# Sums of exponentials over keys: three tiles added together ahead of one set of sums, in a layer of attention and experts

## The reference

```python
xn = _layernorm(x)
q, k = _apply_rope(q, k)                        # q, k, v: (8, 16, 512, 32) from xn
scores = einsum('bhqd,bhkd->bhqk', q, k) / sqrt(32)
scores = where(causal, scores, finfo.min)
attn = softmax(scores, axis=-1)
out = einsum('bhqk,bhkd->bhqd', attn, v)        # then @ Wo.T
# experts: top 2 of 8 by xn @ gate_w.T, y = xn @ W_e.T + b_e, weighted sum of the two
return x + attention(xn) + experts(xn)
```

## Time and profile before

| | us |
|---|---|
| runs shown (3) | 1005.15, 1007.92, 1008.72 |
| median | 1007.92 |
| the profiled execution | 1008.12 |
| its span, first to last instruction | 1006.3 |

### The profile page before, as it was taken

The page is one execution under the profiler, slowest core; times in us unless marked ns, Lnnn a source line. Parts: engine busy times, 40 slices in busy tenths (PEclk is TensorE's granted clock), DMA queues, the critical chain, the costliest instruction groups (busy, mean ns, idle before and its releaser), DMA issues.

```text
span 1006.3 us, 18752 instructions
## 1 busy us (share of the span) xinstructions
PE 932.0 (93%) x6589; PEld 447.7 (44%) x6589; DVE 743.2 (74%) x1322; ACT 435.2 (43%) x711; POOL 565.7 (56%) x557
## 2 busy tenths in 40 slices
PE   2899989989999978988999999989999999999887
PEld 1344434434444433444555555544444444444333
DVE  7888988888889899543444444477878888788865
ACT  5367866666765432331211211214433444334442
POOL 1545675664676548572333333237887788777651
PEclk9999999999999999998999999999999999999999
DMA  6366588788785352385555555554555554455431
GB/s 238 106 220 223 146 278 311 204 300 292 206 291 209 117 210 85 134 309 177 179 168 176 179 170 174 168 214 142 184 159 176 191 191 148 148 181 179 157 107 54
DMA packets 107964, 188.63 MB, mean 187 GB/s; under 512 B 11873, under 2 KB 65249, under 8 KB 102625
## 3 DMA queue, kind: packets, MB, share of 16 engines
q1 hardware_dynamic: 97072, 152.03, 44.5%
q0 software_dynamic: 10800, 35.40, 12.3%
HBM read 117.13 MB, written 70.25 MB: 186 GB/s over the span
## 4 chain that ended last, share of the span: by engine, by line
PE 67%; DVE 12%; DMA 7%; POOL 6%; ACT 4%; issue 3%; SPq 1%; another core or an unknown queue 0%; DVEq 0%; ACTq 0%; POOLq 0%
PE psum L942 18%; PE psum L1027 11%; PE psum L1036 6%; PE psum L1051 6%; PE psum L990 6%; PE psum L977 5%; PE psum L959 5%; PE psum L993 5%; DMA x_in<-x 3%; PE psum L919 3%; DVE top L1463 3%; PE psum L961 2%; POOL gT L571 1%; DMA c_rows<-c_turn 1%; POOL y_in L616 1%
## 5 line engine op out<-in xcount | busy, mean ns | idle before, releaser
L756 ACT ACTIVATE pT<-psum,factors 128x512 f32<-128x512 f32 (+1 forms) x352 | 219.6, 640 | 267.6 <-PE psum L977 239.3
L1463 DVE TENSOR_REDUCE top<-psum 128x1 f32<-128x384 f32 (+3 forms) x352 | 210.7, 635 | 24.1 <-PE psum L961 23.1
L1027 PE MATMUL psum<-xT,w_att 128*128 128x512 f16 x768 | 199.0, 385 | 6.9 <-DVE xT L1414 4.8
L942 PE MATMUL psum<-w_exp,x_gT 128*128 x852 | 197.4, 382 | 0.8 <-DVE x_gT L1419 0.6
L959 PE MATMUL psum<-k_stack,q_stack 96*128 96x384 f16 (+3 forms) x512 | 129.1, 305 | 22.2 <-DVE top L1463 21.4
L606 POOL DMA_INDIRECT x_g<-xn_rows,tok_of x71 | 67.3, 948 | 143.8 <-PE psum L919 136.4
L977 PE MATMUL psum<-q_stack,k_stack 98*128 98x256 f16 (+3 forms) x512 | 129.5, 306 | 6.3 <-ACT pT L756 5.0
L1419 DVE TENSOR_TENSOR x_gT<-psum,x_gT 128x512 f16<-128x512 f32 x71 | 49.0, 692 | 106.9 <-ACT x_gT L780 94.4
L942 PEld LDWEIGHTS psum<-w_exp,x_gT 128*128 128x128 f16 x852 | 83.9, 98 | 87.4 <-issue 3.9
L780 ACT ACTIVATE x_gT<-psum 128x512 f16<-128x512 f32 x71 | 42.3, 597 | 173.2 <-PE psum L919 173.1
L590 POOL TENSOR_SCALAR_AFFINE_SELECT pT<-pT 128x512 f32<-128x512 f32 x128 | 99.3, 785 | 18.7 <-ACT pT L756 18.7
(11 more groups left out here) (172 smaller groups left out, 1283.9 us busy)
## 6 DMA issues: line engine op xcount, KB each, us to landing
y_rows<-y_sb SPq DMA_DIRECT2D x71, 256.0 KB
w_in<-w_all SPq DMA_DIRECT2D x12, 1024.0 KB, 9.6
q_stack<-qk_rows SPq DMA_DIRECT2D x96, 128.0 KB
k_stack<-qk_rows SPq DMA_DIRECT2D x96, 128.0 KB
x_in<-x SPq DMA_DIRECT2D x8, 1024.0 KB, 13.5
qk_rows<-q_hl SPq DMA_DIRECT2D x32, 256.0 KB, 2.2
qk_rows<-k_hl SPq DMA_DIRECT2D x32, 256.0 KB
xn_rows<-x_in SPq DMA_DIRECT2D x8, 1024.0 KB, 4.7
```

The lines of the kernel that those rows point to most:

```text
L756: act.activation(p_of(j, h, heads), banks[BANK_T + (NT_ * n + k) % 2][:, 0:W], ACT.Exp, scale=factors[:, 0:1]).then_inc(exp_done, 1)
L942: now = pe.matmul(banks[s % 4], x_gT[s % 4][:, xp * C + c, :], w_exp[:, bass.ds(e, 1), wp, c, :].rearrange("p e d -> p (e d)"), start=n == ...
L1027: now = pe.matmul(bank, w_att[:, what, wp, c, g * P:(g + 1) * P], xT[b % 2][:, xp * C + c, :], start=at_pass == 0, stop=at_pass == 3 * C - 1)
L1463: return dve.tensor_reduce(out=top[:, h:h + heads, i], in_=banks[BANK_S + k % 2][:, 0:heads * W].rearrange("p (h t) -> p h t", h=heads), a ...
```

## The change

`added(n)` is true for head groups 16 to 30. For these, TensorE makes the sums of tile 0 as before, and leaves the sums of tiles 1, 2 and 3 out of their places. VectorE adds `p_of(2)` and then `p_of(3)` into the right-hand columns of `p_of(1)` (`add_exps`, in the step after, between the second and the third score maximum), once the product of tile 1 with v is done and the tiles are masked. TensorE then makes one set of sums over the 384 columns of `p_of(1)`, behind the product of tile 3 with v, after a wait for VectorE (`p_added`). ScalarE's exponentials of tiles 1 to 3 wait for the whole head group before instead of the same tile of it. On GpSimd the low part of k moves, in steps from 16 on, from behind `mask(n, 1)` and the gathers to behind `mask(n, 3)`.

```diff
@@ -295,6 +295,11 @@
     LATE = [w for n in range(N) for w in late_tiles(n)]
     LATE_AT = {w: i for i, w in enumerate(LATE)}
     assert sorted(LATE) == list(range(NT))
+    def added(n):
+        return N1 <= n < N - 1
@@ -636,7 +641,7 @@
                 mask(n, 1)
                 if n >= N1 and n + 1 < N:
                     gather_y(late_tiles(n + 1)[1])
-                if n + 3 < N:
+                if n < N1:
                     low_qk(1, n + 3)
                 if n in TURN_AT:
                     low_x(TURN_AT[n], 0)
@@ -645,6 +650,8 @@
                 if n in TURN_AT:
                     low_x(TURN_AT[n], 2)
                 mask(n, 3)
+                if n >= N1 and n + 3 < N:
+                    low_qk(1, n + 3)
                 if n in TURN_AT:
                     low_x(TURN_AT[n], 3)
                 if n == CHOOSE + 2:
@@ -752,7 +759,7 @@
                 W = heads * (S - j * P)
                 act.wait_ge(t_done, NT_ * n + k + 1)
                 if n:
-                    act.wait_ge(pv_done, J * (n - 1) + j + 1)
+                    act.wait_ge(pv_done, J * n if added(n - 1) and j else J * (n - 1) + j + 1)
                 act.activation(p_of(j, h, heads), banks[BANK_T + (NT_ * n + k) % 2][:, 0:W], ACT.Exp,
                                scale=factors[:, 0:1]).then_inc(exp_done, 1)
@@ -978,6 +985,12 @@
                                     q_stack[u][0:ROW_C + 2, h0 + h, j * P:S], start=True, stop=True)
                 now.then_inc(t_done, 1)
+            def sums(n, j, last):
+                for h in range(HG):
+                    now = pe.matmul(banks[BANK_DEN][h * HD:(h + 1) * HD, j * P:S], ones32[:], p_of(j, h, 1),
+                                    start=j == 0, stop=j == last)
+                return now
             def times_v(n, j):
                 b, g = n // G, n % G
                 pe.wait_ge(masked, J * n + j + 1)
@@ -987,12 +1000,15 @@
                         pe.wait_ge(o_read, n)
                 W = S - j * P
                 for h in range(HG):
-                    pe.matmul(banks[BANK_O][h * HD:(h + 1) * HD, j * P:S], v_sb[b % 2][:, j, g * P + h * HD:g * P + (h + 1) * HD],
-                              p_of(j, h, 1), start=j == 0, stop=j == J - 1)
-                for h in range(HG):
-                    now = pe.matmul(banks[BANK_DEN][h * HD:(h + 1) * HD, j * P:S], ones32[:], p_of(j, h, 1),
-                                    start=j == 0, stop=j == J - 1)
-                now.then_inc(pv_done, 1)
+                    now = pe.matmul(banks[BANK_O][h * HD:(h + 1) * HD, j * P:S], v_sb[b % 2][:, j, g * P + h * HD:g * P + (h + 1) * HD],
+                                    p_of(j, h, 1), start=j == 0, stop=j == J - 1)
+                if not added(n) or j == 0:
+                    sums(n, j, J - 1).then_inc(pv_done, 1)
+                elif j < J - 1:
+                    now.then_inc(pv_done, 1)
+                else:
+                    pe.wait_ge(p_added, n - N1 + 1)
+                    sums(n, 1, 1).then_inc(pv_done, 1)
             def times_v_last(i, first, last):
@@ -1472,6 +1488,17 @@
                 own.link(dve.tensor_tensor(c_hl[:, 0, :], tops, c_scale[:], ALU.mult))
                 dve.tensor_tensor(c_hl[:, 1, :], c_f[:], c_hl[:, 0, :], ALU.subtract).then_inc(c_made, 1)
+            def add_exps(n):
+                dve.wait_ge(pv_done, J * n + 2)
+                for j in range(2, J):
+                    dve.wait_ge(masked, J * n + j + 1)
+                    W = S - j * P
+                    to = p_of(1).rearrange("p (h t) -> p h t", h=HG)[:, :, S - P - W:S - P]
+                    now = dve.tensor_tensor(to, to, p_of(j).rearrange("p (h t) -> p h t", h=HG), ALU.add)
+                    if j < J - 1:
+                        own.link(now)
+                now.then_inc(p_added, 1)
             def normalise_o(n):
                 dve.wait_ge(pv_done, J * (n + 1))
                 if n in JOB_AT:
@@ -1535,6 +1562,8 @@
                     largest_score(n + 1, 1)
                 if n in NORM_AT:
                     rstd_of(NORM_AT[n])
+                if n and added(n - 1):
+                    add_exps(n - 1)
                 if nxt:
                     largest_score(n + 1, 2)
                     largest_score(n + 1, 3)
```

More of the change, by code:

```diff
@@ L235, in moe_attention_layer @@
     c_loaded = [sem(f"c_loaded{u}") for u in range(3)]
-    t_done, exp_done, masked, pv_done = (sem(n) for n in ("t_done", "exp_done", "masked", "pv_done"))
+    t_done, exp_done, masked, pv_done, p_added = (sem(n) for n in ("t_done", "exp_done", "masked", "pv_done", "p_added"))
     o_read, o_hi, o_lo, wo_done, experts_done, sum_done = (sem(n) for n in ("o_read", "o_hi", "o_lo", "wo_done", "experts_done", "sum_done"))
```

## The result

| | before | after |
|---|---|---|
| median, us (4 runs each, side by side) | 1006.53 (1002.35 to 1008.72) | 1023.59 (1020.87 to 1026.57) |
| the profiled execution | 1008.12 | 1026.57 |
| its span | 1006.3 | 1024.8 |

A forecast was written before the change was run, and what follows sets the result against it. TensorE was taken as the bound, 21.05 us a step over another loop of 20.22. Step 17 +0.55, twelve loops +14.6, last steps +0.58 and +1.66: together 17.4 on 1008.1, giving 1025.5 us, range 1011 to 1035.

The forecast's parts named there:

- Step 1: On TensorE, sums of the third and fourth tiles go: 0.65 us a step in 15 steps, 9.8 us if TensorE stays bound.
- Step 2: On VectorE, the two inserted adds cost 1.95 us as a free pair.
- Step 3: VectorE's adds and GpSimd instructions run one after the other, the waiting engine next; the first add lasts over 1.5 us.
- Step 4: GpSimd's k low part, 1.16 us, precedes the second add either way; SyncE's stores leave 1 to 2 us later, hidden.
- The new loop: One normalise start to the next, through GpSimd's row, adds and two maxima: 22.2 us, with TensorE's own work at 20.40.
- The twelve loops: Normalise of step 17 to that of step 29: twelve loops of 22.2 us, 266.4 against 251.81, +14.6 us.
- the clock's rival: TensorE's clock falls at every new wait: 12 x 1.3 us on top, 1041 us; chance 0.13.
- Steps 30 and 31: Last steps, without rope or k: normalise later by 0.58 us in step 30 and 1.66 us in step 31.
- A sign that failed: TensorE's busy time over the kernel falls by some 10 us while the span grows.
- Step 17: First normalise behind the adds, with GpSimd already free: it starts at 694.45 instead of 693.90, +0.55 us.
- the adds are hidden: Rival: VectorE's adds are hidden and TensorE stays the bound, 998 us; chance 0.09.
- The port gives the adds their turn first: Rival: both VectorE adds go ahead of GpSimd's k low part, or overlap it: loop 21.09 us, total 1012; chance 0.13.

The follow-up runs named there:

- e3: The changed kernel with both adds cut to one column per head, waits and signals kept: 999.91 us, 0.9941 times before.
- e2: The changed kernel with GpSimd starting k's low part only when both adds are done: 1013.61 us, 1.0119 times before.
- e1: The changed kernel with k's low part put back ahead of the masks, adds kept: 1024.09 us, 1.0212 times before.
- e4: The kernel before with only the move of k's low part behind the masks, no adds: 1005.94 us, 1.0000 times before.
- e7: The kernel before with only GpSimd's second pair of gathers moved behind the masks, no adds: 1008.05 us, 0.9992 times before.
- e5: The changed kernel with GpSimd's second pair of gathers behind the masks and k's low part back ahead of them: 1010.54 us, 1.0022 times before.
- e9: As e2, but only the fourth tile is added and the third tile's sums stay on TensorE: 1004.94 us, 0.9983 times before.

## Why the prediction was right, and where it was off

The forecast was 1025.5 us for the profiled execution's 1008.1; it took 1026.57, and the median is 1023.59. The mechanism in a steady step was the forecast's; that the total came so close is in part luck, as the parts below show.

- **Step 1, sums removed:** e3's loop of 20.40 is the predicted 21.05 - 0.65.
- **Step 2, price of the adds:** free pair 1.95 predicted, 1.95 in the chain of e2. The group of second adds in after, over all 15 steps (busy us, mean ns, idle before), is the 692 ns of the earlier trace rows:

```profile
L1497 DVE TENSOR_TENSOR pT<-pT 128x512 f32<-128x512 f32 x15 | 10.4, 692 | 0.5
```

- **Step 3, the shared port:** right for the sum. From 700 to 920 us the first add averages 2.125 us in after and 1.250 in e2, where GpSimd is idle beside it (groups of instructions by form, first of after, then of e2):

```profile
L1497 DVE TENSOR_TENSOR pT<-pT 128x1024 f32<-128x1024 f32 x10 | 21.2, 2125 | 0.0
```
```profile
L1498 DVE TENSOR_TENSOR pT<-pT 128x1024 f32<-128x1024 f32 x10 | 12.5, 1250 | 0.0
```

  The Trainium skill (SBUF — State Buffer, section Summary: rules for kernel authors) has the second of such a pair to issue fully blocked until the first finishes. The timeline of the result agrees: the add issued 0.18 us behind the low part and ended 1.11 behind its end. But the prediction's reading that the engine that waited gets the next turn failed where it was put to the test: in the timeline of after, step 28, the add has waited since 956.59 behind a mask, and the low part queued behind that mask still goes first.

```profile
955.84 1.22 POOL L595 TENSOR_SCALAR_AFFINE_SELECT pT<-pT 128x512 f32<-128x512 f32 x2
956.59 3.41 DVE L1497 TENSOR_TENSOR pT<-pT 128x1024 f32<-128x1024 f32 x2 [0.37 <-POOL pT L595]
957.03 1.15 POOL L591 TENSOR_TENSOR k_hl<-plain_k,k_hl 128x512 f16<-128x512 f32 x1
960.05 1.51 PE L990 MATMUL psum<-pT,ones 128*32 128x384 f32 x8 [2.51 <-DVE pT L1497]
```

  By the chain the first add ends at 959.28, 1.10 behind the low part's end (958.18). The same happened in the step at 889. It changes nothing in the sum, since the low part stands once in the row either way, as step 4 had it.
- **Step 4, the low part stands in the row wherever it is put, and SyncE is hidden:** the first is shown by e1 (21.97 against 21.96), the second fits e4 (1.0000) and e2, where the low part comes later still.
- **The new loop:** 22.2 predicted, 21.96 in an undisturbed step. With the step above, whose N is 827.09 - 21.96 = 805.13, the gathers end at N + 16.81 (16.82 predicted) and the second add at N + 20.98 (946.49 - 925.49 = 21.00 predicted). The miss of 0.24 is the last term: two maxima and the gaps, 1.21 by the records, took 0.98, because a record overlaps its neighbour's on the same engine by some 0.1.
- **The twelve loops:** +14.6 predicted, +14.49 measured, but partly by cancelling: undisturbed loops would have given 12 x 21.96 - 251.81 = +11.7, and three disturbed ones, which the forecast did not have, added the rest. The match of the total is luck to that extent. In the first, a gather is issued 1 us late (timeline of after):

```profile
886.26 1.02 POOL L621 DMA_INDIRECT y_in<-y_rows,idx_y  x1 [1.31 <-issue]
892.76 0.85 PE L990 MATMUL psum<-pT,ones 128*32 128x384 f32 x8 [2.05 <-DVE pT L1497]
```

  Before has the same late issue at 877.57, hidden under TensorE. Now GpSimd is in the loop: 22.66, and TensorE waits 2.05 us. Behind that wait the granted clock is 0.50, that is 1.2 GHz (chain, and windows of 1 us, columns as above):

```profile
894.14 2.56 PE psum L1043 x6
...
894.00:895.00 1.00, 1.00 (x4) 0.38 (x3) 0.93 (x3) 0.69 (x1) 0.83 (x1) 0.50 0.64 214
```

  The half projection takes 2.56 instead of 1.30, and the next loop 23.36, 1.40 more than the ordinary: the price that the prediction gave the clock's rival (1.3). The third is step 28 above, where the sums themselves take 1.51 instead of 0.85 after a wait of 2.51. So the clock's rival is no mechanism of every step, as argued from the earlier trace rows: behind the ordinary wait of 1.34 (826.16) the half projection at 827.33 took its 1.30. It came behind the longer waits.
- **Steps 30 and 31:** the loop to N(30) is 0.38 longer than before's and the loop to N(31) 1.20, together 1.58; the forecast's sum has 0.58 + 1.66 = 2.24. The 1.66 was counted against before's N(31) with N(30) left in its place, so adding both counts 0.58 twice unless the masks move with N(30). They did not: they end at 994.02, 32.40 behind N(29), instead of 33.14. On the other side the sums ahead of N(31) took 1.46 instead of the 0.85 counted.
- **Not foreseen:** from N(31) to the end 27.41 instead of 26.40, 1.0 us. The granted clock is 0.50 from 996 to 999, behind two waits of TensorE close together, 1.11 for a mask and 1.39 for the adds; before's is 1.00 around its N(31). These are the sums and the next group (chain of after):

```profile
995.88 1.46 PE psum L990 x8
997.34 0.97 PE psum L984 x2
```

- **A sign that failed:** TensorE's busy time was to fall by some 10 us. It fell by 2.2 (929.8 against 932.0); in e3 it fell by 10.5 (921.5). The half clock, at which the same matmuls last longer, fits: of the 1 us windows from 690 us on, 15 of after have a granted clock of 0.50 and 7 of before, and from 664 to 690 us 6 and 2. How much of the 8 us it makes wasn't measured.
- **Step 17:** +0.55 was predicted; N(17) came 1.42 later, though the stage's first maxima came 1.72 earlier. Little of that is the change's. From the first maxima to N(17) the two kernels without adds differ by 2.7 us among themselves (30.92 in e4, 28.24 in e7); before has 28.26 and after 31.40. From `add_attention` on, where the adds are, the changed kernel is 0.89 longer (690.53 to 695.32, before 690.00 to 693.90). N(17) lies anywhere from 691.30 to 698.10 in the profiled executions of this document, so the 1.42 can't be put down to the change. Why the stage starts unevenly wasn't tried.

The parts add up: 1.42 + 14.49 + 0.38 + 1.20 + 1.01 = 18.50 us, the difference of the spans. The rivals: "the adds are hidden" fell, since even the free pair gives 21.10 (e2, e5); its stated point of decision, adds of under about 1.4 us, fits e9, whose one add of 0.69 is hidden. "The port gives the adds their turn first" is not what the changed kernel does. Its loop of 21.09 looks like e2's 21.10, but that is a coincidence: 21.09 was GpSimd's row without the low part, while in e2 the masks end at 814.84, 0.13 ahead of the adds, and the step is set by the ring through TensorE and VectorE.

## What to carry to other kernels

A full engine doesn't say what relief of it is worth: ask how long the loop through the other engines is. Here it took 20.22 us under 21.05, read in the one step where the full engine has less to do, so 0.83 us a step was all that relief of TensorE alone could win. Work moved into that loop counts there in full, and with it the GpSimd instruction that holds up the add. Moving k's low part to another place in the row only changed which wait the page names (e1); taking 3.5 us of gathers out of the row won 0.86 us a step, down to the next ring (e5). Move only a piece that fits under the cover: the one add of e9 does, though its gain is too small to be sure of in the time.

## What the runs showed that was not expected

- A VectorE add that waits for a GpSimd instruction doesn't always get the next turn: a GpSimd instruction queued right behind went first, at 889.73 and 957.03, and the add took 2.7 us.
- A second ring lay 0.86 us under the first: TensorE's output projection, `add_attention`, two maxima, the adds, the sums (21.10). Clearing GpSimd's row could not bring more with both adds in that place.
- GpSimd issued one gather 1 us late in this stage (1.31 us ahead of it instead of 0.27) in every kernel here, with no cause shown. What it costs depends on how far GpSimd's row is behind the ring that sets the step: nothing in before, 0.44 us in e2, 0.67 in e3, and in the changed kernel 0.7 in that loop and, through the clock, 1.4 in the next.
